# Layers 2 and 3 attention of an eight-stage network: the low part of the keys made in the cycle that projects them

## What is computed

```python
q = (x @ Wq).reshape(B, Nq, HEADS, DIM_HEAD)
k = (context @ Wk).reshape(B, context.shape[1], HEADS, DIM_HEAD)
v = (context @ Wv).reshape(B, context.shape[1], HEADS, DIM_HEAD)
sim = jnp.einsum('bihd,bjhd->bhij', q, k) * SCALE
attn = jax.nn.softmax(sim, axis=-1)
out = jnp.einsum('bhij,bjhd->bihd', attn, v)
return out.reshape(B, Nq, HEADS * DIM_HEAD) @ Wo + bo
```

## Time and profile before

| | us |
|---|---|
| runs of the kernel before: lowest, median, highest of 3 | 1435.8, 1440.9, 1441.27 |
| profiled execution, its own time | 1438.69 |
| its span, first to last instruction | 1436.4 |
| granted TensorE clock, mean over the span | 0.986 |
| share of the span: PE, PEld, DVE, ACT, POOL | 95%, 71%, 70%, 66%, 52% |
| layer 2 attention | 518 to 766 |
| layer 3 attention | 908 to 1402 |

### The profile page before, as it was taken

One profiled execution on the slowest core, in us unless ns is written; L12 is line 12 of the kernel. 1 busy time (PEld: TensorE's weight loads), 2 busy tenths in 40 slices (PEclk: granted clock), 3 DMA queues, 4 the chain that ended last, 5 costly groups with the idle time before them and its releaser, 6 DMA issues. The chain is left out here.

```text
span 1436.4 us, 30044 instructions
## 1 busy us (share of the span) xinstructions
PE 1365.3 (95%) x9799; PEld 1013.6 (71%) x9799; DVE 1004.6 (70%) x2375; ACT 941.8 (66%) x1951; POOL 745.3 (52%) x763
## 2 busy tenths in 40 slices
PE   7999989998998989999999999999999999999988
PEld 5555558897664867777775777677777777777767
DVE  6877856778667667777776566577767767777683
ACT  4787776785667547676664465576766667676654
POOL 5455641111762236666665486465656656565542
PEclk9999999999999999999999999899999999999999
DMA  6300000000001300000001000000000000000003
GB/s 174 83 0 0 1 8 23 1 1 1 1 1 48 89 0 1 2 0 0 0 0 38 1 0 2 0 1 1 1 0 0 0 0 0 0 0 0 1 3 87
DMA packets 31516, 20.55 MB, mean 14 GB/s; under 512 B 9569, under 2 KB 29000, under 8 KB 31432
## 3 DMA queue, kind: packets, MB, share of 16 engines
q1 hardware_dynamic: 31204, 19.38, 4.9%
q10 hardware_dynamic: 228, 0.10, 0.0%
HBM read 18.42 MB, written 1.05 MB: 14 GB/s over the span
## 5 line engine op out<-in xcount | busy, mean ns | idle before, releaser
L2368 POOL TENSOR_TENSOR arena<-arena,l3a_rinv 128x512 f32<-128x512 f32 x256 | 260.3, 1040 | 200.5 <-DVE l3a_rinv L2767 200.1
L2662 ACT ACTIVATE arena<-l3a_scores_ps,l3a_nmax 128x512 f32<-128x512 f32 x256 | 174.8, 685 | 125.2 <-DVE l3a_nmax L2761 125.0
L2368 POOL TENSOR_TENSOR arena<-arena,l2a_rinv 128x512 f32<-128x512 f32 x128 | 129.9, 1039 | 91.0 <-DVE l2a_rinv L2767 90.8
L2761 DVE TENSOR_REDUCE l3a_nmax<-l3a_scores_ps 128x2 f32<-128x1024 f32 x128 | 155.8, 1218 | 20.3 <-PE l3a_scores_ps L2441 20.3
L874 ACT ACTIVATE l0a_prob<-l0a_scores_ps,l0a_k_scale 128x1024 f32<-128x1024 f32 x128 | 135.5, 1112 | 34.6 <-PE l0a_scores_ps L724 33.9
L2472 PE MATMUL l3a_work_ps<-l3a_probT,l3a_v 128*64 128x256 f32 x1024 | 124.6, 385 | 3.1 <-DVE l3a_probT L2773 3.1
L2662 ACT ACTIVATE arena<-l2a_scores_ps,l2a_nmax 128x512 f32<-128x512 f32 x128 | 87.4, 686 | 60.2 <-DVE l2a_nmax L2761 60.1
L2773 DVE COPY l3a_probT<-l3a_scores_ps 128x512 f32<-128x512 f32 x65 | 44.9, 691 | 96.1 <-PE l3a_scores_ps L2449 96.0
L2472 PEld LDWEIGHTS l3a_work_ps<-l3a_probT,l3a_v 128*64 128x64 f32 x1024 | 67.8, 136 | 52.1 <-issue 19.5
L2761 DVE TENSOR_REDUCE l2a_nmax<-l2a_scores_ps 128x2 f32<-128x1024 f32 x64 | 77.7, 1217 | 9.5 <-PE l2a_scores_ps L2441 9.5
L738 PE MATMUL l0a_pv_ps<-l0a_prob,l0a_v 128*32 128x256 f32 x1024 | 70.2, 392 | 0.0
(11 more groups left out here) (778 smaller groups left out, 3823.6 us busy)
## 6 DMA issues: line engine op xcount, KB each, us to landing
l1f_w<-in_L_ffn_w SPq DMA_DIRECT2D x16, 256.0 KB, 2.8
arena<-in_ctx SPq DMA_DIRECT2D x4, 384.0 KB, 5.4
w_l_w<-in_L_ffn_W SPq DMA_DIRECT2D x1, 1024.0 KB
arena<-in_L_ffn_W SPq DMA_DIRECT2D x16, 64.0 KB, 1.9
out_x<-x_tokens SPq DMA_DIRECT2D x8, 128.0 KB, 1.9
x_tokens<-in_x SPq DMA_DIRECT2D x1, 896.0 KB, 7.4
const<-in_constants SPq DMA_DIRECT2D x1, 525.0 KB
w_l_wo<-in_L_xattn_Wo SPq DMA_DIRECT2D x1, 512.0 KB
```

The source lines that it names most:

```text
L2368: e.tensor_tensor(prob[n][:, :], prob[n][:, :], bcast(rinv[:, n:n + 1], [P, S]), ALU.mult).then_inc(m.prob_ready, 1)
L2662: e.activation(prob[at][:, :], scores_bank(b, c, u), ACT.Exp, bias=nmax[:, at:at + 1], accum_out=rsum[:, at:at + 1]).then_inc(m.exp_ready, 1)
L2761: e.tensor_reduce(nmax[:, at:at + 2], sps[:, first:first + 1024].rearrange("p (h k) -> p h k", h=2), AX.X, ALU.max, negate=True).then_inc( ...
```

## The change

Two places of the VectorE program of `wide_attention`:

```diff
                     maxima(b, c, 0)
-                    if c + 1 < C or more:
-                        k_low(*((b, c + 1) if c + 1 < C else (b + 1, 0)))
+                    if c == 2 and first:
+                        k_low(0, 3)
                     maxima(b, c, 1)
...
                     if turns_here:
                         keep_turned(*turn_c, 0, turned_bank(b, c, 0))
+                    if onward:
+                        k_low(*on)
                     invert(b, c, 1)
```

## The result

The changed kernel is slower by 0.4%, about half of what was forecast. Over 20 runs each its median is 1442.63 us (1440.45 to 1445.46) against 1436.37 us (1432.02 to 1441.96) for the kernel before. The ratio is 1.0044, with a 95% interval from 1.0032 to 1.0057, so 4.6 to 8.2 us. The forecast was 1451, with a range from 1443 to 1458. The three runs of before that the prediction had to go by were at the upper side of the twenty.

The account below looks back on a forecast made before the run. TensorE was taken as the bound in both stages. Net costs 6.6 + 1.1 + 3.0 + 0.5 = 11.2 us on 1438.7 gave 1449.9, or 1452.1 against the runs' median; forecast 1451, range 1443 to 1458.

Parts of the forecast that it names:

- The part taken away: Cycle 3, TensorE's turning of finished tokens: its waits for k_low go, saving some 6.0 us together.
- Who waits for the maxima: Cycle 3: ScalarE's exponentials, then keep_z, then TensorE's key projection wait for them; the projection waits 0.85 us.
- The step that failed: VectorE, ordinary batches: k_low in the invert's place makes cycle 3's first maxima 0.51 later; 6.6 us over 13 batches.
- The join of layer 2: Layer 2's join, three cycles after cycle 3, waits for q_low because VectorE still lags; 0.15 x 7 = 1.1 us.
- The lag behind cycle 3: VectorE's lateness after cycle 3: 0.73 us, shrinking by only 0.07 a cycle.
- First batches: First batch of each layer: k_low delays the key projection and then weighted; 1.52 us each, 3.0 us together.
- Last batch of layer 3: Cycles 4 and 5: k_low delays the copy behind the second invert, mostly regained; 0.5 us, between 0 and 1.4.
- The bound loop: Rival: the VectorE and ScalarE loop exceeds TensorE's 7.17 us, lengthening ordinary cycles by 0.1; 1455 to 1460, chance 0.12.
- The absorbed lag: Rival: new wait about as long as the old, only first batches cost; 0 to 5 us, 1439 to 1446, chance 0.13.

Follow-up runs that it names:

- kernel 6: Changed kernel with apply moved ahead of the first copy of turned tokens, in VectorE's gap; 1436.23 us, ratio 1.0003 to the kernel before.
- kernel 7: Changed kernel with the second invert moved behind apply in the cycle with the join; 1437.52 us, ratio 1.0007 to the kernel before.
- kernel 10: Changed kernel with the second invert moved ahead of the first copy in the cycle with the join; 1435.66 us, ratio 0.9993 to the kernel before.
- kernel 3: Changed kernel with k_low one place later, behind the second copy of turned tokens; 1436.95 us, ratio 1.0015 to the kernel before.
- kernel 8: Kernel before with apply in VectorE's gap and the first batches' late apply early too; 1430.22 us, ratio 0.9960 to the kernel before.
- kernel 11: Changed kernel with apply and the first batches' late apply both moved early; 1431.63 us, ratio 0.9963 to the kernel before.
- kernel 9: Kernel before with the second invert one place later, behind the second copy, in the cycle with the join; 1444.97 us, ratio 1.0052.

## Why the prediction was right in direction and wrong in size

- **The part taken away.** Right. The waits for k_low went, in all 15 places, and the next block starts at weighted + 1.87.
- **Who waits for the maxima.** Right. The new wait is on keep_z, at L2410, 13 times, and from 1.94 on each 0.1 us on the maxima is 0.1 us on the cycle: 1.94, 2.28 and 2.56 give 7.68, 8.02 and 8.30. Below that there is slack, since at 1.52 and less the cycle is 7.35.
- **The step that failed**: "So the copy, q_low, apply and the first maxima of cycle 3 all come 0.51 later". It took apply's 1.41 us for VectorE's own work and moved it as a block. Of that time 0.60 is work, as kernels 6, 7 and 10 show; the rest was waiting for GpSimd's scaling, to whose end the maxima were tied. The invert came 0.60 later, as forecast, and with it the scaling. The maxima came 0.34 later: in the kernel before one operation of apply was still to run when the scaling ended (maxima at 1119.27, 0.26 behind 1119.01), while in the changed kernel the first of the two got through between the two multiplies and only one was left (1124.20, together with the scaling's end). 0.60 - 0.26 = 0.34, and 4.3 us where 6.6 stood. The same tie also took k_low's cost away in kernel 3, and apply's place was the larger prize that the prediction did not see. The prediction says of the later scaling that it costs nothing, which holds for TensorE, which reads its results, and not for VectorE, which ran beside it.
- **The join of layer 2.** 1.1 us forecast, nothing measured. The lag behind cycle 3 is 0.51 (maxima 1.52 us behind the scores, 1.01 without lag), not 0.73, and shrinks by 0.16 a cycle, not by 0.07: 1.52, 1.36, 1.21. In the loop the invert and the copy behind it are 0.08 apart (1121.92, 1122.00), not 0.17; the 0.26 between them in the earlier trace rows held a wait of the copy for TensorE.
- **First batches.** 3.0 forecast, 3.0 measured, and in part by luck: 1.52 was forecast for each and they took 1.75 and 1.27. The waits are those forecast: turned unit 2 waits for keep_o (0.89) and weighted for the copy (0.6 and 0.5). But the maxima of cycle 3 came 1.10 and 0.69 later, not 0.9, since the late apply was blocked here too, and kernels 8 and 11 show that without this k_low costs cycle 3 only 0.15 and nothing. In layer 3:

```profile
942.03 1.09 PE L2449 MATMUL l3a_work_ps<-const,arena 128*128 128x128 f32 x8 [0.89 <-DVE arena L2778]
...
944.51 0.69 DVE L2755 TENSOR_TENSOR l3a_k_lo<-l3a_turned_ps,l3a_k_hi 128x512 fp32r<-128x512 f32 x1 [1.88 <-ACT l3a_k_hi L2651]
```

- **Last batch of layer 3.** 0.5 forecast, 0.9 by the cycles, of which 0.31 is in its last cycle, and that one takes 9.6 to 10.6 us in the thirteen traces, whatever the kernel. The 0.6 in cycle 5 is in every kernel in which the k_low of cycle 4 stands ahead of the second copy; in kernel 3, where it stands behind it, cycle 5 takes 8.24 as before.
- **The rivals.** The bound loop did not come. The absorbed lag was right in its result (up to 1446) and not in its mechanism: the new wait costs the cycle 0.34 more than the old one did.

With 4.3, 0, 3.0 and 0.9 the sum is 8.2, and 1438.7 + 8.2 = 1446.9. Against the median of 20 runs it is 1444.6, 2 us above the measured one and at the upper end of the measured 4.6 to 8.2; what makes up these 2 us stays open. So of the 8.4 us between the forecast of 1451 and the measured 1442.6, 3.0 are costs that were put too high (11.2 for 8.2), 2.0 are this rest, and 3.4 are the starting point: 1451 less 11.2 is 1439.8, and the median of twenty runs is 1436.4.

## What to carry to other kernels

Before a duration is moved with its instruction, compare it with the shortest of its kind in the trace. An operation that takes 1.15 us here and 0.34 there is waiting inside, for an engine that no list of waits names, and what moves its end is what moves that engine. A short instruction that releases GpSimd (here a 0.15 us invert) decides when such work of VectorE runs freely, so ask of every such release what VectorE does in the next microseconds. Two waits of the bounding engine close behind each other may be one lateness seen twice: removing the first then only feeds the second.

## What the hardware showed that was not expected

**Blocked operations.** Apply is blocked during GpSimd's multiplies, and can get in between two of them. The two multiplies of a scaling take 1.04 us each, the second starting 1.00 behind the first. In the thirteen traces an operation of apply starts 106 times while the first of such a pair runs. The 61 that start 0.28 us or more ahead of its end (0.29 in the changed kernel, 0.89 in kernel 9, 967 ns for the first operation) get in between the two. The 45 that start 0.12 us or less ahead of it (0.07 in the kernel before: started at 1117.94, the first multiply ends at 1118.01) do not, and wait for the second multiply too, 1148 to 1201 ns in all. Starts between 0.12 and 0.28 did not occur, and why the start decides it stays open. A multiply takes 1.03 to 1.06 us in every case, so that all of the loss was VectorE's.

**TensorE's clock at the start of a stage.** The stretch of the first scores of layer 2, in the kernel before and in the changed one (window: length, busy (x) by engine, granted clock, DMA share, GB/s):

```profile
520.00:523.00 3.00, 3.00 (x16) 2.02 (x17) 1.22 (x1) 0.00 (x0) 0.00 (x0) 0.60 0.00 0
```

```profile
521.00:524.00 3.00, 3.00 (x21) 2.24 (x20) 1.80 (x3) 0.98 (x2) 0.00 (x0) 1.00 0.00 0
```

Between the stages TensorE has gaps: from 514 to 517 (before) and from 515 to 518 (changed) it was busy for 2.05 and 1.82 us, at a granted clock of 0.76 and 0.84. In the next 3 us, up to the windows shown, it was busy throughout, at 0.50 and 0.59, so the clock was at its 1.2 GHz level for all or most of them. The first scores start at 519.73 and 520.76, so the clock goes back to the 2.4 GHz level inside them (before) or ahead of them (changed). In layer 3 it is the same: the first scores start at 910.21 and 913.36, and the clock is still 0.50 from 910 to 911 before, and 0.99 from 913 to 914 in the changed kernel. The first cycle of layer 2 takes 6.0 to 6.2 us where it is back in time and 7.2 where it is not; layer 3's takes 5.4 or 5.9 to 6.1. In layer 2 both came with kernels that differ in nothing ahead of it, so a single trace carries up to 1.8 us of this kind, and a change of a few us is better read from the cycles it touches than from two spans.
